# Mixture-of-experts block on one core: token-expert pairs sorted into tiles of one expert each, with the positive part of the routed tiles taken by DVE from PSUM

## The reference, cut to what matters

```python
# x: 4096 tokens x 256; E = 8 experts, K = 2 per token, H = 64 hidden, ITERS = 2, DT = 0.1
def _inl(ctrl, xs, vs, mu):
    a, b, g = split(ctrl, 3)                       # ctrl has 768 columns
    v_next = sigmoid(a) * vs - softplus(b) * (xs - mu)
    return xs + DT * sigmoid(g) * v_next, v_next

probs = softmax(gelu(x @ router_w1 + b) @ router_w2 + b)
topk_p, topk_i = top_k(probs, 2)                   # normalised to sum 1
v, integrated = 0, x
for _ in range(2):
    ctx = concat(integrated, v)                    # 512 wide
    shared_ctrl = gelu(ctx @ shared_w1 + b) @ shared_w2 + b
    x_sh, v_sh = _inl(shared_ctrl, integrated, v, mu)
    ctrl = [gelu(ctx @ w1[e] + b1[e]) @ w2[e] + b2[e] for the 2 experts e of each token]
    x_r, v_r = _inl(ctrl, integrated, v, mu), weighted by topk_p and summed
    x_next, v_next = sw * (x_sh, v_sh) + (1 - sw) * (x_r, v_r)
    halt = sigmoid(gelu(integrated @ halt_w1 + b) @ halt_w2 + b)
    integrated, v = integrated + halt * (x_next - integrated), v + halt * (v_next - v)
refined = gelu(integrated @ refine_w1 + b) @ refine_w2 + b
out = layernorm(x + (x + integration_weight * refined))
```

## Time and profile before

| what | us |
|---|---|
| median of 3 runs | 1670.16 |
| the profiled execution | 1671.22 |
| its span, first to last instruction | 1669.5 |
| attention, up to the first instruction of `experts` | 594 |
| `FIRST` with its loads | 594 to 727 |
| one turn of `ROUND` (two groups through all three stages) | about 256 |
| `LAST` | 1494 to 1669.5 |
| PE busy over the span | 1355.1 (81%) |
| DVE busy | 1121.7 (67%) |
| ACT busy | 827.3 (50%) |
| POOL busy | 518.6 (31%) |

### The profile page before, as it was taken

The page is one execution under the profiler, slowest core; times in us unless marked ns, Lnnn a source line. Parts: engine busy times, 40 slices in busy tenths (PEclk is TensorE's granted clock), DMA queues, the critical chain, the costliest instruction groups (busy, mean ns, idle before and its releaser), DMA issues.

```text
span 1669.5 us, 22624 instructions
## 1 busy us (share of the span) xinstructions
PE 1355.1 (81%) x7776; PEld 726.9 (44%) x7776; DVE 1121.7 (67%) x2038; ACT 827.3 (50%) x1429; POOL 518.6 (31%) x490
## 2 busy tenths in 40 slices
PE   4778877888889827889978789988789987789964
PEld 2334543545445413345533345543345543345532
DVE  1665665566667245977768687777677678677683
ACT  1134543345545524655655555555556555556543
POOL 6112313123223313323432314442314252314242
PEclk9678998899989958999988899988899998899986
DMA  4957176382670050000000000000000000000000
GB/s 83 154 66 122 48 94 105 56 121 56 85 111 19 26 153 1 1 0 1 3 12 26 1 15 1 1 13 26 1 15 1 1 13 11 16 13 1 1 0 26
DMA packets 83216, 62.54 MB, mean 37 GB/s; under 512 B 27633, under 2 KB 82185, under 8 KB 83090
## 3 DMA queue, kind: packets, MB, share of 16 engines
q1 hardware_dynamic: 83090, 60.92, 20.8%
HBM read 39.63 MB, written 20.97 MB: 36 GB/s over the span
## 4 chain that ended last, share of the span: by engine, by line
PE 36%; DVE 16%; ACT 5%; issue 4%; SPq 1%; POOL 1%; DMA 1%; POOLq 0%; DVEq 0%; ACTq 0%
PE exp_ps L1782 19%; DVE x L1569 5%; PE exp_ps L1688 4%; PE exp_ps L1690 4%; PE exp_ps L1689 4%; DVE ctrl L1558 2%; PE exp_ps L1677 2%; DVE onehot L1488 2%; PE exp_ps L1728 1%; ACT gp L1338 1%; SPq L1141 1%; PE exp_ps L1719 1%; DVE top_f L1484 1%; DVE sp L1556 1%; DVE ctrl L1553 1%
## 5 line engine op out<-in xcount | busy, mean ns | idle before, releaser
L1782 PE MATMUL exp_ps<-w,routed 128*128 128x512 f16 (+1 forms) x2304 | 442.2, 346 | 1.6 <-DVE routed L1536 1.6
L1289 POOL TENSOR_TENSOR sp<-sp,ctrl 128x768 f32<-128x768 f32 x64 | 124.5, 1945 | 645.4 <-ACT ctrl L1348 645.4
L1782 PEld LDWEIGHTS exp_ps<-w,routed 128*128 128x128 f16 x2304 | 226.7, 99 | 199.8 <-issue 12.2
L563 DVE TENSOR_REDUCE neg_max<-att_ps 128x1 f32<-128x512 f32 (+3 forms) x448 | 216.9, 533 | 71.4 <-PE att_ps L732 69.5
L501 ACT ACTIVATE probs<-att_ps 128x512 f32<-128x512 f32 x320 | 175.5, 609 | 168.3 <-PE att_ps L741 167.3
L1361 ACT ACTIVATE ctrl<-exp_ps 128x512 f32<-128x512 f32 (+1 forms) x192 | 137.2, 715 | 195.3 <-PE exp_ps L1782 194.8
L731 PE MATMUL att_ps<-k_stack,q_stack 96*128 96x512 bf16 (+3 forms) x512 | 161.1, 356 | 69.8 <-DVE neg_max L563 32.5
L1544 DVE TENSOR_SCALAR ctrl<-ctrl 128x768 uint32<-128x768 uint32 x64 | 67.9, 1061 | 125.9 <-ACT ctrl L1361 125.8
L1569 DVE SCALAR_TENSOR_TENSOR x<-ctrl,nwx,x 128x256 f32<-128x256 f32 x192 | 145.7, 759 | 3.4
L741 PE MATMUL att_ps<-q_stack,k_stack 98*128 98x512 bf16 (+3 forms) x512 | 124.6, 317 | 8.3 <-DMA q_stack<-max_parts 5.8
L732 PE MATMUL att_ps<-mask_q,identb 128*128 128x128 bf16 x512 | 125.5, 251 | 0.0
(11 more groups left out here) (204 smaller groups left out, 2517.4 us busy)
## 6 DMA issues: line engine op xcount, KB each, us to landing
parts_dram<-parts SPq DMA_DIRECT2D x48, 256.0 KB, 2.6
q_stack<-parts_dram SPq DMA_DIRECT2D x96, 128.0 KB, 6.0
k_stack<-parts_dram SPq DMA_DIRECT2D x96, 128.0 KB, 9.4
x_in<-in_L_attn_encodings SPq DMA_DIRECT2D x8, 512.0 KB, 10.6
normed_dram<-normed SPq DMA_DIRECT2D x8, 512.0 KB, 11.2
x<-normed_dram SPq DMA_DIRECT2D x8, 512.0 KB, 3.9
out<-final SPq DMA_DIRECT2D x8, 512.0 KB, 2.9
ctrl<-in_L_ffn_expert_w SPq DMA_DIRECT2D x1, 1536.0 KB, 8.4
```

The lines of the kernel that those rows point to most:

```text
L563: return v.tensor_reduce(out, scores, AX.X, ALU.max, negate=True)
L1289: gp_.tensor_tensor(sp[:, t], sp[:, t], ctrl[:, t, :, D:2 * D], ALU.subtract).then_inc(pool_step, 1)
L1782: last = t_.matmul(ctrl_ps(s)[:, a - cols[0][0]:z - cols[0][0]], stationary, moving[:, a:z], start=(j == 0), stop=(j == len(terms) - 1))
```

## The change

`attention` stays. `experts` is written anew, without loops, in five phases, each over all tokens:

1. Router: all 8 groups through router, halt and shared hidden layer (`rr`, `rs`, `rl`), before anything else.
2. Sort: DVE computes from the choices the place `pos` of each of the 8192 token-expert pairs in an array of 72 tiles of 128, in which each tile holds pairs of one expert only (the last tile of an expert is padded). POOL scatters the tokens' rows there with 64 indirect DMAs (`xs_dram`). Beside it the shared stream of iteration 1 (`W_S1`).
3. Iteration 1, routed (`W_B`): 18 quads of 4 sorted tiles. They are loaded, turned, sent through the expert's own 64 hidden units (a tile's expert number is loaded into a register of PE and addresses the weights) and its own second layer, and their results are stored to `rs1_dram`.
4. Iteration 2: POOL gathers for each token the two results (64 indirect DMAs), DVE adds them up (`combine1`); the shared stream of iteration 2 (`W_S2`) with the halt gate; x and v go to `xv_dram` and are gathered again in sorted order (72 indirect DMAs) for 18 quads (`W_D`), whose results go to `rs2_dram`.
5. Refinement: 64 more gathers, `combine2`, and the old stage 3 for 8 groups.

A second layer takes two operand pairs for every stream now (high and low part stacked on 128 rows), not 13. Element-wise work is done in blocks of four tiles of one stream, 128 x 1024. In the routed quads the positive part of b is no longer taken by ACT, but by DVE from PSUM (`relus`), behind ACT's tanh of the same slot (`tanh_slot`); the shared blocks keep it on ACT. mu is subtracted once from x.

```diff
-            def mask(st, k, c):
-                dst, done = ring(st, f"mask{k}{c}")
-                t_.matmul(dst, spread[:, c, :], onehotT[st.g][:, k, :], start=True, stop=True).then_inc(done, 1)
...
+            def control_tile(dst, it, hl, h1, w_at):
+                parts = ((0, 2 * D), (2 * D, CTRL)) if it == 2 else ((D, CTRL),)
+                for j, (stationary, moving) in enumerate(((hl, w2_top), (h1, w2_low))):
+                    for a, z in parts:
+                        last = t_.matmul(dst[:, a - parts[0][0]:z - parts[0][0]], stationary,
+                                         moving[:, ds(w_at + a, z - a)], start=(j == 0), stop=(j == 1))
+                return last
...
+            def quad_experts(q):
+                return [pe.value_load(tile_expert[0:1, q * NT + i:q * NT + i + 1], min_val=0, max_val=E - 1)
+                        for i in range(NT)]
...
+            for q in range(QUADS):
+                if q + 1 < QUADS:
+                    turn_sorted2(q + 1)
+                control(W_D + q, h_hl, h_h1, offsets(es))
+                if q + 1 < QUADS:
+                    es = quad_experts(q + 1)
+                    ready("d", q + 1, 2 * KC)
+                    routed_hidden(f"dh{q + 1}", 2 * KC, es)
...
+            for t in range(TILES):
+                for k in range(2):
+                    g_.indirect_dma_start(xs_dram, IndirectOffsetOnAxis(pos[:, 2 * t + k:2 * t + k + 1], 0),
+                                          xs[:, t, :], None).then_inc(scattered[t // NT], 16)
+            def products(n, x):
+                par = n % 2
+                b = ct[:, par, :, D:2 * D] if it_of(n) == 2 else ct[:, par, :, 0:D]
+                m = rb[:, par, :, D:]
+                pool.wait_ge(ln_done, n + 1)
+                g_.tensor_tensor(m, m, b, ALU.subtract).then_inc(pool_step, 1)
+                pool.wait_ge(pool_step, n - W_B + 1)
+                g_.tensor_tensor(m, m, x, ALU.mult).then_inc(mul_done, 1)
...
+            def gather_state(q):
+                if q >= 3:
+                    pool.wait_ge(ew_done, W_D + q - 3 + 1)
+                for t in range(NT):
+                    g_.indirect_dma_start(xg_it2(q)[:, t, :], None, xv_dram,
+                                          IndirectOffsetOnAxis(ids[:, q * NT + t:q * NT + t + 1], 0)
+                                          ).then_inc(gx_full[q % 3], 16)
...
+            for q in range(QUADS):
+                products(W_D + q, xg_it2(q)[:, :, 0:D])
+                if q + 3 < QUADS:
+                    gather_state(q + 3)
...
+            for q in range(QUADS):
+                if q + 1 < QUADS:
+                    casts("d", q + 1, 2 * KC)
+                tanhs(W_D + q)
+                logs(W_D + q)
+                if q + 1 < QUADS:
+                    gelu_hidden(W_D + q + 1, f"dh{q + 1}", h_hl[:], False)
...
+            def relus(n):
+                par, it = n % 2, it_of(n)
+                if n - 2 >= W_B and not is_shared(n - 2):
+                    dve.wait_ge(rs_stored[par], 16 * (stores_before(n - 2, par) + 1))
+                for u in range(uses(n), uses(n + 1)):
+                    i = u - uses(n)
+                    dve.wait_ge(tanh_slot[u % 2], slot_turn(u))
+                    if it == 1:
+                        raw = slot_ps(u).rearrange("p (t n) -> p t n", t=2)
+                        m, b = rb[:, par, 2 * i:2 * i + 2, D:], raw[:, :, 0:D]
+                    else:
+                        m, b = rb[:, par, i, D:], slot_ps(u)[:, D:2 * D]
+                    v.tensor_scalar(m, b, 0.0, None, ALU.max).then_inc(ctrl_freed[u % 2], 1)
...
+            for q in range(QUADS):
+                if q + 1 < QUADS:
+                    lows("d", q + 1, 2 * KC)
+                relus(W_D + q)
+                absolute(W_D + q)
+                if q:
+                    velocity(W_D + q - 1, xg_it2(q - 1)[:, :, D:])
+                if q + 1 < QUADS:
+                    hidden(W_D + q + 1, f"dh{q + 1}", h_hl, h_h1)
...
+            for g in range(GROUPS):
+                if g + 1 < GROUPS:
+                    lows("c", g + 1, 2 * KC)
+                absolute(W_S2 + g)
+                weigh(g)
+                if g + 2 < GROUPS:
+                    combine1(g + 2)
+                if g:
+                    velocity(W_S2 + g - 1, vs[:, (g - 1) * NT:g * NT, :])
+                    add_shared2(g - 1)
+                if g + 1 < GROUPS:
+                    hidden(W_S2 + g + 1, f"cs{g + 1}", h_hl, h_h1)
+                    halts(g + 1)
```

More of the change, by code:

```diff
@@ L1294, in _, with then @@
-            stages(pool, stage)
+            g_ = nc.gpsimd
+            def then():
+                pool.wait_ge(const_step, steps.next())
+            g_.memset(w2rh[:], 0.0).then_inc(consts, 1)
+            g_.memset(ident[:], 1.0).then_inc(const_step, 1)
+            then()
+            g_.affine_select(out=ident[:], in_=ident[:], compare_op=ALU.is_equal, fill=0.0,
+                             base=0, pattern=[[-1, P]], channel_multiplier=1).then_inc(const_step, 1)
+            then()
+            g_.memset(zeros[:], 0.0).then_inc(zeros_ready, 1)
@@ new lines, in products @@
+            def products(n, x):
[6 more added lines that the diff above has]
+                g_.tensor_tensor(m, m, x, ALU.mult).then_inc(mul_done, 1)
+            for q in range(QUADS):
+                products(W_B + q, xg_it1(q)[:, :, 0:D])
@@ new lines, in stream_weights @@
+            def stream_weights(tiles, it):
+                n = tiles.stop - tiles.start
+                v.tensor_scalar(halt[:, tiles], gates_t[:, tiles, 1], -0.025, -0.025, ALU.mult, ALU.add).then_inc(dve_step, 1)
+                then()
+                v.tensor_tensor(nwx[it][:, tiles, :], weights[:, tiles, :],
+                                halt[:, tiles].unsqueeze(2).to_broadcast([P, n, STREAMS]), ALU.mult).then_inc(dve_step, 1)
+                then()
+            dve.wait_ge(gates_done, 1)
@@ new lines, in add_shared2 @@
+            def add_shared2(g):
+                n = W_S2 + g
+                dve.wait_ge(ew_done, n + 1)
+                dve.wait_ge(xv_stored[g], 32)
+                for t in range(NT):
+                    tt = g * NT + t
+                    last = v.scalar_tensor_tensor(xs[:, tt, 0:D], rb[:, n % 2, t, 0:D], nwx[1][:, tt, 0:1],
+                                                  xs[:, tt, 0:D], ALU.mult, ALU.add)
+                last.then_inc(acc_done, 1)
+            combine1(0)
+            lows("c", 0, 2 * KC)
@@ new lines, in _, with combine2 @@
+            velocity(W_D + QUADS - 1, xg_it2(QUADS - 1)[:, :, D:])
+            def combine2(g):
+                for t in range(g * NT, (g + 1) * NT):
+                    dve.wait_ge(cb2_full[t % CB2S], 32 * (t // CB2S + 1))
+                    for k in range(2):
+                        last = v.scalar_tensor_tensor(xs[:, t, 0:D], cb2(t)[:, k, :], nwx[1][:, t, k + 1:k + 2],
+                                                      xs[:, t, 0:D], ALU.mult, ALU.add)
+                        if k == 0:
+                            last.then_inc(dve_step, 1)
+                            then()
+                    last.then_inc(comb_done, 1)
@@ L1649, in _ @@
[L1649 to L1656 removed]
+            combine2(0)
+            lows("e", 0, KC)
+            combine2(1)
+            dve.wait_ge(rf_in, 16 * 3)
@@ L1658, in _ @@
+            v.tensor_scalar(iw, iw, 0.5, None, ALU.mult).then_inc(dve_step, 1)
+            then()
+            for g in range(GROUPS):
+                if g:
+                    lows("e", g, KC)
+                    steps = spread_of(g - 1)
+                refine_low(g)
+                if g:
+                    finish(g - 1, steps)
+                take(g)
+                if g + 2 < GROUPS:
+                    combine2(g + 2)
+            finish(GROUPS - 1, spread_of(GROUPS - 1))
         @block.tensor
@@ L1844, in _ @@
-            transpose_state(Stage(FIRST, 0, None))
-            stages(pe, stage)
+            SHARED_AT = [E * CTRL] * NT
+            pe.wait_ge(w2_ready, 1)
+            pe.wait_ge(rows_in, 16 * 9)
+            control(W_S1, hl_all[:, 0, :], hl_all[:, 1, :], SHARED_AT)
+            pe.wait_ge(onehot_ready, 1)
+            oh = onehot[:].rearrange("p j e -> p (j e)")
+            dst, done = ring("rank")
+            t_.matmul(dst, before[:], oh, start=True, stop=True).then_inc(done, 1)
+            dst, done = ring("tot")
```

1659 lines of the change are left out of this document (909 added, 750 removed).

## The result

The changed kernel took 1953.11 us (median of 4; 1946.22 to 1956.4), the kernel before 1672.58 beside it: a ratio of 1.166, 95% interval 1.161 to 1.172. The sign was as forecast, the size was not: 281 us slower in the place of 120, and 13 us above the end of the range. The profiled execution took 1946.22, its span 1944.5.

A forecast was written before the change was run, and what follows sets the result against it. The old kernel was taken as close to a PE bound, DVE right behind; the new one as bound by chains and serial stretches. Phases summed to 1195 us in place of 1075, span 1789, forecast 1790; range 1620 to 1940, likeliest 1700 to 1880.

The forecast's parts named there:

- What is removed: PE's second layer loses 372 us, and most hidden layers of seven unchosen experts go besides; PE no longer sets the end.
- That is a loop: 4 G + 4.8 + 3.6 ... PE's needs are below that as well: Routed iteration 2: POOL's four gathers, products and velocity set each quad, 14.5 us with handovers; ACT's chain of 11.3 hides.
- D: Routed quads of iteration 2: 17 x 14.5 = 246 us, ending at 1552.
- B, "12": Routed quads of iteration 1: 9.7 us chain plus 2.4 for a POOL product in DVE's way, 12 a quad, 204 in all.
- the walk: Forecast's method: one quad or group followed through each phase and the phases added, each beginning only when the one before ended.
- G = 1.3: Price in us of one indirect DMA on POOL, taken near SP's strided loads at 1.13; bounds .45 and 2.4.
- Rival 2: Scatter and gathers: indirect DMAs cost 2.4 us each, as when they wait for DVE; total 1969 us; chance 0.16.
- phase C: Shared stream of iteration 2: DVE sets 21.4 us a group, POOL's 15.2 hides; 8 groups, 171 us.
- phase E: Refinement: 22.6 us a group, all handovers; seven times that and 10 for `combine2`, 168 us.
- Rival 3: Stages overlap, each phase going by its busiest engine; 1604 us, faster than before; decides from 1653 down; chance 0.22.
- The serial stretches: Router start, sort, scatter and phase changes: 48 + 39 + 19 + 85 + 53 + 27 + 54 = 325 us the old kernel lacked.
- PE's busy share near 50%, a clock below 0.83 in B and D: Expected signs: PE busy about half of 1790 us, its granted clock below 0.83 in both routed phases.

The follow-up runs named there:

- velocity first: Changed kernel with DVE doing the previous quad's velocity ahead of the low parts, positive parts and signs in both routed phases; 1872.78 us, ratio 1.118.
- the run with numbers loaded ahead: Changed kernel with positive part on ACT; iteration 1: five buffers, POOL products after next hidden layer; iteration 2: velocity cut in two; expert numbers before transposes; 1798.51 us.
- the run with all edits and the positive part on DVE: Changed kernel with five buffers in iteration 1, iteration 2's velocity cut in two, POOL products after next hidden layer, expert numbers before transposes; 1788.31 us, ratio 1.070.

## Why the prediction was wrong, by its own steps

- **What is removed** was right for the second layer: its matmuls kept PE busy for 502 us before (L1782) and 175 now (L1971), 327 less where the forecast had 372. "And most of the hidden layers of seven unchosen experts besides" was wrong: the routed hidden layers (L2062 to L2065) keep PE busy for 130 us; before it was some 137 (an estimate: four of five parts of the 171 us that L1688 to L1690 took with `w`). 1440 matmuls of 128 columns stand in the place of 576 of 512. With 94.8 us of transposes of sorted tiles new, PE's busy time fell by 247 us net, which did not shorten the kernel.
- **"That is a loop: 4 G + 4.8 + 3.6 ... PE's needs are below that as well"** is the step that failed. I looked for loops on one engine's program (POOL's gathers, velocity, products) and for each engine's own need. The circle through three buffers crosses SP or POOL, DMA, PE, ACT and DVE. All its terms stood in my text: gathers 5, landing 4, transposes and casts, tanh, positive part, signs, velocity 3.6. I used the landing of 4 us at the phase starts only. Added up for D from the chain above: 3.8 until the last gather starts, its landing 3.7, transposes 3.4, second layer and tanh 4.6, positive part and signs 1.0, velocity 3.6, handovers .4: 20.5, not 14.5. PE's rows ahead of the prediction show the transposes ahead of the second layer, and the diff shows `velocity(q - 1)` behind `relus(q)`. I did not put the two together. It is longer than the forecast's loop by 17 x 6.1 = 104 us of D's 109. Opening it alone gave back only 39 of them, for a second circle I had not looked for either (velocity, low parts, positive part, PE's slot) takes 18.4 us.
- **B, "12"**: same step for the greater part. 14.7 was measured, and 12.6 to 12.8 as soon as the circle was open (two ways), which gave back 38 and 33 of B's 48.5 us. The rest is the walk's own chain, short by .8 a quad: PE had .9 in it and took 3.6.
- **G = 1.3** was right: .96 and a gap of .30. It had come from SP's strided loads, another engine's issue, so there was luck in it.

```profile
L1288 POOL DMA_INDIRECT xs_dram<-xs,pos x64 | 67.7, 1058 | 121.3 <-DVE pos L1713 102.1 <-issue 19.2
...
L1328 POOL DMA_INDIRECT xg<-xv_dram,ids x72 | 70.8, 984 | 187.8 <-DVE rb L1751 170.6 <-issue 17.2
```

64 of them fill 87 of the scatter's 88.5 us. In D, POOL stood idle for 171 us until L1751, the velocity: the row that gives the circle away.
- **Rival 2** was named with the right neighbourhood in time (1969) and the wrong cause. The Trainium skill, SBUF — State Buffer, § SBUF: two separate sides, lets one expect a DMA of GpSimd's queue to be starved while DVE runs in a 2-port mode. In phase C, with DVE busy for 159 of 208 us, no gather of results took over 1.02 us (median .947), so that phase does not show it; which of DVE's operations ran in such a mode no run here tells. But DVE did hold some indirect DMAs. Durations in ns, least, median and greatest, of the scatter:

```profile
L1288 POOL DMA_INDIRECT xs_dram<-xs,pos x64: 956/961/2150, 763.0 to 848.9; - x64
```

  Seven of the 64 took 1.54 us and one 2.15, and each of the eight lay across the end of DVE's L1760 and the start of its L1762, two operations of 1.22 us with two operands from SBUF; the run with velocity first has the same eight. In phase E a few gathers took up to 1.41. For the scatter that adds 5 us, where the rival asked for 1.1 on each of 264.
- **Rival 3** (overlap): refuted for this order. Nor did the orders tried reach it; B came to 10 to 11 us where it had 7.9, D never below 14.3 where it had 12.5.
- **The serial stretches** (A 169, scatter 88.5) and C and E were sized within 8% each. The range's upper end was taken from the price of one unknown operation. It should have been taken from the chance that a loop had been overlooked in the phases that make up half the sum.
- **"PE's busy share near 50%, a clock below 0.83 in B and D"**: 57%, and .69 and .73. In B each refill made PE idle for 8 us; the eight transposes behind it took 1.97, as in the earlier trace rows, and the second layer .43 a matmul of 512 columns (the 1.2 GHz level), then .22 (2.4 GHz). The forecast counted that at the starts of phases only. By an estimate from these rows and from 16 transposes in 1.94 us at the upper level (velocity first, 1510.75), it is up to 1.5 us of a quad of B inside the circle.

## What to carry to other kernels

When a kernel goes from one engine's bound to chains, walk each ring of buffers round once: from the operation that frees a buffer, through refill and first reader, to the next operation that frees one, following each engine's program order; the longest such circle divided by the quads it spans is the phase's pace. Where a wait disappears, look at what now stands ahead of others on the engine to which work was moved. A cost per operation (.42 or .38 us for the positive part) says little: moving it from DVE to ACT changed the time by -9, -56, +16 and +6 us in four orders of the rest. Only the -56 is well clear of noise; in the other three pairs the intervals overlap. Work that is counted away (here every expert but the chosen ones) must be priced again in its new shape: for the hidden layer, matmuls a quarter as wide saved PE next to nothing.

## What the runs showed of the hardware

- An indirect DMA of 128 rows, 1 or 2 KB each, holds POOL for .95 us and is followed by a gap of .30; it lands 2.5 to 4.2 us later (medians of scatter and gathers). Scatter and gathers agree within .02 us, and most are not slowed by a busy DVE; across two DVE operations with two SBUF operands each it took 1.54, and once 2.15.
- A load of a number from SBUF into a register of PE costs .64 us of PE's program, four of them 2.5 us (chain of the run with numbers loaded ahead: 2.57). With weights addressed by those registers, the 52 matmuls of a hidden layer in D took 4.8 us; with constant addresses they took 3.1 (both at the 2.4 GHz level, positive part on ACT, numbers loaded ahead).
- A DVE copy of 64x512 halves (.28 us alone) waits up to 2.4 us behind a POOL product, like the operations with two operands; the positive part from PSUM (.42, or .69 for 512 columns) and the low parts (.69) were never held up beside one: .693 at most, for 29 and 66 of them that began inside a product in the run with all edits and the positive part on DVE.
